# A transformer chain on one core: LayerNorm of the wide attention and of the router, taken as centred weights and a scale

## The chip, the cores and the metric

One core of a Trainium2 chip runs the whole program. The metric is the time on the device in microseconds (us), from one launch; smaller is better. The engines are TensorE (PE; its weight loads are listed as PEld), VectorE (DVE), ScalarE (ACT), GpSimd (POOL) and SyncE (SP, which here issues most DMAs).

## The reference, cut to what matters

32 samples of 128 tokens with 256 features pass through four pairs of cross attention and feed-forward. Each block takes the LayerNorm of the state (no gain, no offset) and is added with a gate:

```python
def _layernorm(x, axis=-1, eps=1e-05):
    m = jnp.mean(x, axis=axis, keepdims=True)
    v = jnp.var(x, axis=axis, keepdims=True)
    return (x - m) / jnp.sqrt(v + eps)

x = x + tanh(g_xattn[1]) * _L1_xattn_ref(_layernorm(x), ctx, w_q, w_k, w_v, w_out, b_out)
x = x + tanh(g_ffn[1])   * _L1_ffn_ref(_layernorm(x), router_w, router_b, expert_w, expert_b)
```

The wide attention (L1) has 16 heads of 64: queries `norm(x) @ w_q`, keys and values from the context, `softmax(q k^T / 8)`, then the output matrix. The mixture behind it picks one of eight experts per token: `logits = norm(x) @ router_w + router_b`, its softmax maximum is the weight, and the chosen expert's matrix is applied to `norm(x)`.

## The kernel before, in words

Four lanes (one sample each) run interleaved. A lane goes through the stages L0 (narrow cross attention), bit (a ternary feed-forward with a convolution), L1 (wide attention) and route (the router) for its 8 passes; then through mix, L2, self and L3 for 8 passes; at the end eight lanes run the last feed-forward. Each stage is written per engine as a generator whose `yield`s cut it into turns, and one string per engine (`ORDER`) says which lane has the next turn. So the order on each engine is fixed, and an engine that waits in one turn holds up every later turn of all lanes. The strings come from a planner outside the kernel.

A LayerNorm (`dve_norm`) is `st` and `ag` on DVE (mean and variance), `var` and `rstd` on POOL (lines 1464 and 1466), then `xn` on DVE (line 785): `(x - mean) * rstd`. PE transposes `xn` (`pe_normed`, the helper's line is 403), ACT copies the result to `xnT`, and the matmuls use that.

In L1 a lane does two halves of eight heads: scores in two PSUM banks, DVE's maximum over 128x1024 (line 839) and `shift` (line 842), eight exponentials on ACT (line 1346, each 128x128 with the row sum as accumulator), a reciprocal per four heads on DVE (`rc`, line 847), the normalisation on POOL (`n`, line 1506), the transposes on PE (line 423), values, output matrix, and an add to the state (`x0`, `x1`, line 854). The exponential and its shift are:

```python
dve.tensor_scalar(top, top, -WIDE ** -0.5, None, ALU.mult)
last = act.activation(t.e[half][:, j, :], t.ab[:, half, j * S:(j + 1) * S], ACT.Exp, scale=WIDE ** -0.5,
                      bias=t.tiny[:, 8 + h:9 + h], accum_out=t.tiny[:, 40 + h:41 + h])
```

In route, `xn` is used twice: by the router's matmul, whose logits get the bias in `lg` (line 950), and by the experts, for which SP sends it to DRAM (`mixture_in`, line 1736). The semaphore `kept` counts the DMAs of the state and of `mixture_in`; the next pass's L0.xn on DVE and L0 `xb` on POOL wait for it, since they overwrite `xn` and `x`. The next pass's keys on PE may start once `lg` has read its bank.

In some passes a lane also computes a tile of the experts (`pe_tile`, `dve_norm`'s `tile.y`) inside these stages. The set-up's constants are turns of a fifth lane; lane 0 starts after them, since its second bank serves as their PSUM bank (`setup_bank`). Up to `bias_L1` they prepare the ternary weights and the output matrices.

## Time and profile before

| | us |
|---|---|
| timed runs, median of 3 | 2629.39 (2628.02 to 2634.43) |
| profiled execution | 2608.25 |
| its span from first to last instruction | 2607.0 |
| PE busy in the span | 2456.1 (94%) |
| DVE busy | 2012.0 (77%) |
| ACT busy | 1666.9 (64%) |
| POOL busy | 1136.2 (44%) |

Busy times are of the profiled execution, whose time is 21 us under the median of the timed runs. Matmuls are pipelined and their ends are modelled, so a busy PE is not a PE at its peak. The first half (L0, bit, L1, route) lies before about 1230 us, the second half behind it, with an overlap of some tens of us.

### The profile page before, as it was taken

To read this page: it belongs to the slowest core of one execution; us is meant where nothing else is said; L and a number is where in the kernel's file an instruction comes from. 1 tells how busy PE (TensorE), PEld (TensorE's weight loads), DVE (VectorE), ACT (ScalarE), POOL (GpSimd) and SP (SyncE) were. 2 spreads that over 40 slices of the span, in tenths; PEclk is the share of its full clock that TensorE was granted. 3 is DMA by queue.
4 is the path that set the end of the run, shared out by engine and by line. 5 is a ranking of instruction groups with operands and counts; after the bars stand their busy time and mean duration, and the time that the engine had idled before them with its cause. 6 is when DMAs were issued, how large, how long until landed. Compare 5 with 4: busy or idle time off the path is not lost.

```text
span 2607.0 us, 66544 instructions
## 1 busy us (share of the span) xinstructions
PE 2456.1 (94%) x26500; PEld 2019.9 (77%) x26500; DVE 2012.0 (77%) x4666; ACT 1666.9 (64%) x4539; POOL 1136.2 (44%) x1989
## 2 busy tenths in 40 slices
PE   6898989898899989999999999999999999999999
PEld 5687867687677777787778878788887878788887
DVE  7778787878688695977586667778777676868998
ACT  4676766777676766676566566666666565656544
POOL 3233423333544544334654554434343433345776
PEclk8898989999999999999999999999999999999999
DMA  6000000000011221000011321100000100000111
GB/s 204 6 24 9 22 10 26 10 20 16 22 48 58 74 60 50 26 24 22 26 55 43 92 76 42 40 20 20 12 27 16 29 16 23 26 6 11 45 32 35
DMA packets 84189, 92.50 MB, mean 35 GB/s; under 512 B 15332, under 2 KB 77288, under 8 KB 83880
## 3 DMA queue, kind: packets, MB, share of 16 engines
q1 hardware_dynamic: 75432, 59.91, 7.4%
q0 software_dynamic: 8448, 28.34, 3.8%
q8 instruction: 210, 3.44, 0.6%
q14 instruction: 99, 0.81, 0.1%
HBM read 65.36 MB, written 22.85 MB: 34 GB/s over the span
## 4 chain that ended last, share of the span: by engine, by line
PE 57%; DVE 23%; ACT 7%; POOL 7%; issue 4%; DMA 2%; SPq 0%; DVEq 0%; POOLq 0%; ACTq 0%
PE psum L375 13%; PE psum L368 10%; PE psum L452 6%; PE psum L403 6%; PE psum L423 5%; DVE tiny L801 3%; PE psum L468 3%; PE psum L596 3%; DVE big L810 3%; PE psum L382 2%; PE psum L396 2%; PE psum L389 2%; PE psum L590 2%; DVE big L891 2%; DVE xn L785 2%
## 5 line engine op out<-in xcount | busy, mean ns | idle before, releaser
L1303 ACT ACTIVATE big<-big 128x512 f32<-128x512 f32 x512 | 313.0, 630 | 155.7 <-DVE big L810 153.3
L801 DVE TENSOR_REDUCE tiny<-psum 128x8 f32<-128x1024 f32 x256 | 311.3, 1219 | 61.0 <-PE psum L452 58.5
L1464 POOL TENSOR_SCALAR tiny<-mv 128x1 f32<-128x1 f32 x224 | 53.4, 238 | 672.2 <-DVE mv L775 670.4
L810 DVE TENSOR_TENSOR big<-psum,tiny 128x512 f32<-128x512 f32 x512 | 335.7, 682 | 4.6
L452 PE MATMUL psum<-head_keys,small 64*128 64x256 f32 x2048 | 286.6, 402 | 17.1 <-ACT big L1265 8.0
L423 PEld LDWEIGHTS psum<-ident,big 64*128 64x128 f32 x5120 | 206.7, 141 | 104.5 <-ACT big L1303 33.1
L423 PE MATMUL psum<-ident,big 64*128 64x64 f32 x5120 | 246.3, 232 | 37.6 <-POOL big L1506 18.6
L1481 POOL TENSOR_TENSOR head_keys<-big,head_rows 128x512 f32<-128x512 f32 x256 | 266.2, 1051 | 0.3
L1265 ACT ACTIVATE big<-psum 128x512 f32<-128x512 f32 x384 | 212.2, 600 | 57.6 <-PE psum L423 54.4
L1506 POOL TENSOR_TENSOR big<-big,tiny 128x512 f32<-128x512 f32 x128 | 134.9, 1058 | 224.5 <-DVE tiny L847 224.2
L452 PEld LDWEIGHTS psum<-head_keys,small 64*128 64x128 f32 x2048 | 182.1, 191 | 63.2 <-ACT big L1265 17.8
L1346 ACT ACTIVATE big<-psum,tiny 128x128 f32<-128x128 f32 x512 | 181.1, 380 | 28.0 <-DVE tiny L842 27.5
L403 PE MATMUL psum<-ident,small 128*128 128x128 f32 x896 | 157.6, 285 | 12.5 <-DVE small L819 4.3
L1265 ACT ACTIVATE head_keys<-psum 128x512 f32<-128x512 f32 x256 | 140.5, 598 | 37.2 <-PE psum L423 36.1
L785 DVE TENSOR_SCALAR xn<-x,mv,tiny 128x256 f32<-128x256 f32 x192 | 103.4, 539 | 74.7 <-POOL tiny L1466 73.8
L403 PEld LDWEIGHTS psum<-ident,small 128*128 128x128 f32 x896 | 100.7, 142 | 51.1 <-DVE small L819 10.9
L1466 POOL TENSOR_TENSOR tiny<-tiny,minus_half 128x1 f32<-128x1 f32 x224 | 129.8, 579 | 18.6
L368 PE MATMUL psum<-xnT,w_L 128*128 128x128 f32 x1024 | 129.7, 277 | 0.8 <-ACT xnT L1333 0.6
L368 PE MATMUL psum<-xnT,w_up 128*128 128x128 f32 x1024 | 130.0, 278 | 0.1
L596 PE MATMUL psum<-w_L,head_keys 128*128 128x256 f32 x512 | 129.0, 390 | 0.7 <-ACT head_keys L1355 0.5
L368 PEld LDWEIGHTS psum<-xnT,w_L 128*128 128x128 f32 x1024 | 123.4, 192 | 5.4 <-ACT xnT L1333 1.9
L368 PEld LDWEIGHTS psum<-xnT,w_up 128*128 128x128 f32 x1024 | 121.3, 192 | 2.8 <-issue 0.9
(339 smaller groups left out, 6473.9 us busy)
## 6 DMA issues: line engine op xcount, KB each, us to landing
ctxT<-in_ctxT SPq DMA_DIRECT2D x64, 128.0 KB, 2.3
after_L_xattn<-x SPq DMA_DIRECT2D x64, 128.0 KB, 1.7
mixture_out<-spare SPq DMA_DIRECT2D x46, 128.0 KB, 2.0
x_in<-in_x SPq DMA_DIRECT2D x32, 128.0 KB, 2.2
mixture_in<-xn SPq DMA_DIRECT2D x32, 128.0 KB, 1.7
x_in<-after_L_xattn SPq DMA_DIRECT2D x32, 128.0 KB, 2.1
w_bits<-after_L_xattn SPq DMA_DIRECT2D x32, 128.0 KB, 2.1
spare<-in_L_w SPq DMA_DIRECT2D x2, 1024.0 KB, 7.2
```

The lines of the kernel that those rows point to most:

```text
L368: last = pe.matmul(bank[:, j * S:(j + 1) * S], wt[:, k, n * P:(n + 1) * P], src[:, k, :], start=k == 0, stop=k == KD - 1)
L375: last = pe.matmul(bank[:, 0:n], srcT[:, k, :], wt[:, k, 0:n], start=k == 0, stop=k == chunks - 1)
L403: last = pe.transpose(bank[:, k * P:(k + 1) * P], src[:, k * P:(k + 1) * P], identity)
L423: last = pe.transpose(t.ab[:, half, at:at + P // 2], t.e[c][rows, j, :], m.ident[rows, rows])
L452: last = pe.matmul(t.ab[:, half, cols], t.qT[rows, r, :], keys[rows, cols], start=l != "self", stop=l != "self" or cols.start > 0)
L596: last = pe.matmul(t.b[:, 0:D], t.kT_wide[:, k, :], m.w["L1o"][:, CH * r + k, :], start=k == 0, stop=k == CH - 1)
L801: dve.tensor_reduce(top, s8, AX.X, ALU.max).then_inc(*t.dve.tell(p, f"{l}.top{r}"))
L810: dve.tensor_tensor(t.e[half], s8[:, mine, :], top[:, mine].rearrange("p (h o) -> p h o", o=1).to_broadcast([P, CH, S]), ALU.subtract).the ...
L1265: return act.activation(dst.rearrange("p h (r s) -> p h r s", r=2), src, ACT.Copy)
L1303: last = act.activation(flat, flat, ACT.Exp, scale=DH ** -0.5)
L1346: last = act.activation(t.e[half][:, j, :], t.ab[:, half, j * S:(j + 1) * S], ACT.Exp, scale=WIDE ** -0.5, bias=t.tiny[:, 8 + h:9 + h], ac ...
L1481: pool.tensor_tensor(t.head_keys[r], t.kT[:, r:r + 1, :].to_broadcast([P, CH, S]), m.head_rows[:].rearrange("p (h o) -> p h o", o=1).to_br ...
```

## The change

The LayerNorm of L1 and of route is no longer applied to the tokens. At set-up PE sums each column of the query matrix and of the router over its 256 rows (a matrix of ones times the weights: `sum_q0`, `sum_q1`, `sum_r`), and DVE subtracts the column's mean from the weights (`mid_q0`, `mid_q1`, `mid_r`), so that the mean of a token drops out of the product. PE then transposes the state `x` itself (`pe_direct`, after `bit.x` or `L1.x1`). The deviation is applied later: in L1 as the exponential's scale, a [128, 1] tensor with rstd / 8 (POOL multiplies the variance by 64 first), and in `shift`; in route as a factor in `lg`. L1's `xn` on DVE is gone; that of route, which the experts need, moves behind `one`, the last step of the router. POOL's `xb` of L1 waits for PE's transposes of `x` instead of `xn`. Where L1 carries a tile, its `tile.y` comes behind `ag` as before, and PE waits for it ahead of the queries. Lane 0 starts after `mid_r` instead of `bias_L1`; the other lanes' first L1 waits for `mid_q1`.

The order strings of all engines are written anew. Counted in turns along them: on PE three more (3627 for 3624), on DVE 29 fewer (3934 for 3963); most turns stand within 10 places of where they stood, once the fewer turns of DVE are counted off. Distance from L1's last output to the router's transposes on PE: median 7 turns before, 4 now; from the router's matmul to the lane's next L0 keys 5 before, 7.5 now; from L1's scores to their transposes 11 before and now; on DVE from route.xn to the lane's next L0.xn 14 to 41 (median 21) before, 4 to 21 (median 7.5) now, in five of 28 places 4 or 5.

```diff
STAGE = {
     "L1": {
         "pe": "kv0 xnT q0 s0 T0 pv0 out0 q1 kv1 s1 T1 pv1 out1",
-        "dve": NORM["dve"] + " top0 shift0 rc0 rc1 x0 top1 shift1 rc2 rc3 x1",
+        "dve": "st ag top0 shift0 rc0 rc1 x0 top1 shift1 rc2 rc3 x1",
         "act": "k0 v0 xnT q0 p0 p1 eT0 eT1 oT0 q1 k1 v1 p2 p3 eT2 eT3 oT1",
         "pool": NORM["pool"] + " xb n0 n1 n2 n3",
     },
...
     },
     "route": {
         "pe": "xnT rt",
-        "dve": NORM["dve"] + " lg mx sub hot hmx one",
+        "dve": "st ag lg mx sub hot hmx one xn",
         "act": "xnT ex",
         "pool": NORM["pool"] + " inv wt",
     },
...
     "pool": "var rstd " + " ".join(f"hb{b} var{b} rstd{b}" for b in range(BLOCKS)),
 }
 SETUP = {
-    "pe": "o_L0 mean o_L1",
-    "dve": "ident fold_L0 bias_L0 abs clip deq r1 r2 r3 w1 s1 s2 w2 fold_L1 bias_L1 plan",
+    "pe": "o_L0 mean o_L1 sum_q0 sum_q1 sum_r",
+    "dve": "ident fold_L0 bias_L0 abs clip deq r1 r2 r3 w1 s1 s2 w2 fold_L1 bias_L1 mid_q0 mid_q1 mid_r plan",
     "act": "tanh",
     "pool": "fill diag band consts first grid",
 }
...
 
 ORDER = {
     "pe": (
...
     ),
     "dve": (
...
     ),
     "act": (
...
     ),
     "pool": (
...
     ),
     "sp": (
...
     ),
 }
 
...
     yield
 
 
+def pe_direct(pe, m, t, p, l, before):
+
+    pe.wait_ge(*t.dve.at(p, before))
+    transposes(pe, t.a, t.x, KD, m.ident[:]).then_inc(*t.pe.tell(p, f"{l}.xnT"))
+    yield
+
+
 def pe_cross(pe, m, t, p, l):
     if l == "L0":
         pe.wait_ge(t.loaded_c, 16 * p + 16)
...
     yield
     pe.wait_ge(*t.act.at(p, f"{l}.v0"))
     yield from pe_tile(pe, m, t, p, l)
-    yield from pe_normed(pe, m, t, p, l)
+    yield from pe_direct(pe, m, t, p, l, "bit.x")
     pe.wait_ge(*t.act.at(p, f"{l}.xnT"))
+    if tile_of(t.n, p, l):
+        pe.wait_ge(*t.dve.at(tile_of(t.n, p, l)[2], "tile.y"))
     for r in range(2):
         chunks = range(CH * r, CH * (r + 1))
         features_T(pe, t.a if r else t.b, m.w["L1q"], t.xnT, chunks[:2])
...
 
 
 def pe_route(pe, m, t, p, l):
-    yield from pe_normed(pe, m, t, p, l)
+    yield from pe_direct(pe, m, t, p, l, "L1.x1")
     if p == 0:
-        pe.wait_ge(m.loads["router"], m.loaded["router"])
+        pe.wait_ge(*m.s.dve.at(0, "setup.mid_r"))
     pe.wait_ge(*t.act.at(p, f"{l}.xnT"))
     tokens(pe, t.b, t.xnT, m.w["router"], E1).then_inc(*t.pe.tell(p, f"{l}.rt"))
     yield
...
 
 def pe_lane(pe, m, t):
     if t.n == 0:
-        pe.wait_ge(*m.s.dve.at(0, "setup.bias_L1"))
+        pe.wait_ge(*m.s.dve.at(0, "setup.mid_r"))
     for p in range(PASSES_A):
         yield from pe_cross(pe, m, t, p, "L0")
         if p == 0:
             pe.wait_ge(*m.s.dve.at(0, "setup.w2"))
         yield from pe_bitlinear(pe, m, t, p, "bit")
         if p == 0:
-            pe.wait_ge(*m.s.dve.at(0, "setup.bias_L1"))
+            pe.wait_ge(*m.s.dve.at(0, "setup.mid_q1"))
         yield from pe_wide(pe, m, t, p, "L1")
         yield from pe_route(pe, m, t, p, "route")
     for p in range(PASSES_A):
...
     pe.wait_ge(*m.s.dve.at(0, "setup.fold_L1"))
     pe_fold(pe, m, "L1", m.setup_bank).then_inc(*m.s.pe.tell(0, "setup.o_L1"))
     yield
+    for n, before in enumerate(("bias_L1", "mid_q0")):
+        pe.wait_ge(*m.s.dve.at(0, f"setup.{before}"))
+        for k in range(KD):
+            last = pe.matmul(m.setup_bank, m.ones[:], m.w["L1q"][:, k, n * BANK:(n + 1) * BANK],
+                             start=k == 0, stop=k == KD - 1)
+        last.then_inc(*m.s.pe.tell(0, f"setup.sum_q{n}"))
+        yield
+    pe.wait_ge(m.loads["router"], m.loaded["router"])
+    pe.wait_ge(*m.s.dve.at(0, "setup.mid_q1"))
+    for k in range(KD):
+        last = pe.matmul(m.setup_bank[:, 0:E1], m.ones[:], m.w["router"][:, k, :], start=k == 0, stop=k == KD - 1)
+    last.then_inc(*m.s.pe.tell(0, "setup.sum_r"))
+    yield
 
 
 def pe_lora(pe, m, t, p, l):
...
     yield
 
 
+def dve_moments(dve, t, p, l):
+
+    dve.bn_stats(t.stats[:], t.x[:]).then_inc(*t.dve.tell(p, f"{l}.st"))
+    yield
+    dve.wait_ge(*t.dve.at(p, f"{l}.st"))
+    dve.bn_aggr(t.mv[:], t.stats[:]).then_inc(*t.dve.tell(p, f"{l}.ag"))
+    yield
+
+
 def dve_wide(dve, m, t, p, l):
-    yield from dve_norm(dve, m, t, p, l, t.x[:], t.xn[:])
+    yield from dve_moments(dve, t, p, l)
+    if tile_of(t.n, p, l):
+        k = tile_of(t.n, p, l)[2]
+        dve.wait_ge(*t.pe.at(k, "tile.y"))
+        dve.tensor_tensor(t.xg, t.b[:, 0:D], t.bg, ALU.add).then_inc(*t.dve.tell(k, "tile.y"))
+        yield
     s8 = t.ab.rearrange("p r (h s) -> p (r h) s", s=S)
     top = t.tiny[:, 8:16]
     for r in range(2):
...
         dve.tensor_reduce(top, s8, AX.X, ALU.max).then_inc(*t.dve.tell(p, f"{l}.top{r}"))
         yield
         dve.wait_ge(*t.dve.at(p, f"{l}.top{r}"))
-        dve.tensor_scalar(top, top, -WIDE ** -0.5, None, ALU.mult).then_inc(*t.dve.tell(p, f"{l}.shift{r}"))
+        dve.wait_ge(*t.pool.at(p, f"{l}.rstd"))
+        dve.tensor_scalar(top, top, t.tiny[:, 1:2], -1.0, ALU.mult, ALU.mult).then_inc(*t.dve.tell(p, f"{l}.shift{r}"))
         yield
         for half in range(2):
             mine = t.tiny[:, 40 + CH * half:40 + CH * (half + 1)]
...
         dve.wait_ge(*t.dve.at(p, f"{l}.{name}"))
 
     dve.wait_ge(*t.dve.at(p, "L1.x1"))
-    yield from dve_norm(dve, m, t, p, l, t.x[:], t.xn[:])
+    yield from dve_moments(dve, t, p, l)
     if p == 0:
         dve.wait_ge(m.loads["router"], m.loaded["router"])
         dve.wait_ge(*m.s.dve.at(0, "setup.plan"))
     dve.wait_ge(*t.pe.at(p, f"{l}.rt"))
-    yield from then(dve.tensor_tensor(lg, t.b[:, 0:E1], m.w["rb"][:], ALU.add), "lg")
+    dve.wait_ge(*t.pool.at(p, f"{l}.rstd"))
+    yield from then(dve.scalar_tensor_tensor(lg, t.b[:, 0:E1], t.tiny[:, 1:2], m.w["rb"][:], ALU.mult, ALU.add), "lg")
     yield from then(dve.tensor_reduce(mx, lg, AX.X, ALU.max), "mx")
     yield from then(dve.tensor_scalar(lg, lg, mx, None, ALU.subtract), "sub")
     yield from then(dve.scalar_tensor_tensor(wt, lg, 0.0, m.first_of[:], ALU.is_equal, ALU.mult), "hot")
     yield from then(dve.tensor_reduce(mx, wt, AX.X, ALU.max), "hmx")
     dve.tensor_scalar(m.hots[sample // MIX][:, sample % MIX, :], wt, mx, None, ALU.is_equal
                       ).then_inc(*t.dve.tell(p, f"{l}.one"))
+    yield
+    dve.tensor_scalar(t.xn[:], t.x[:], t.mv[:, 0:1], t.tiny[:, 1:2], ALU.subtract, ALU.mult
+                      ).then_inc(*t.dve.tell(p, f"{l}.xn"))
     yield
 
 
...
     dve_fold(dve, m, "L1").then_inc(*m.s.dve.tell(0, "setup.fold_L1"))
     yield
     dve_bias(dve, m, "L1")
+    yield
+    for n in range(2):
+        dve.wait_ge(*m.s.pe.at(0, f"setup.sum_q{n}"))
+        for k in range(KD):
+            mine = w["L1q"][:, k, n * BANK:(n + 1) * BANK]
+            last = dve.scalar_tensor_tensor(mine, m.setup_bank, -1.0 / D, mine, ALU.mult, ALU.add)
+        last.then_inc(*m.s.dve.tell(0, f"setup.mid_q{n}"))
+        yield
+    dve.wait_ge(*m.s.pe.at(0, "setup.sum_r"))
+    for k in range(KD):
+        last = dve.scalar_tensor_tensor(w["router"][:, k, :], m.setup_bank[:, 0:E1], -1.0 / D, w["router"][:, k, :],
+                                        ALU.mult, ALU.add)
+    last.then_inc(*m.s.dve.tell(0, "setup.mid_r"))
     yield
     dve.wait_ge(*m.s.pool.at(0, "setup.grid"))
     dve.tensor_scalar(m.before[:], m.causal[:], 0.0, None, ALU.is_le)
...
             act.wait_ge(*t.dve.at(p, f"{l}.shift{r}"))
             for j in range(CH):
                 h = CH * half + j
-                last = act.activation(t.e[half][:, j, :], t.ab[:, half, j * S:(j + 1) * S], ACT.Exp, scale=WIDE ** -0.5,
+                last = act.activation(t.e[half][:, j, :], t.ab[:, half, j * S:(j + 1) * S], ACT.Exp, scale=t.tiny[:, 1:2],
                                       bias=t.tiny[:, 8 + h:9 + h], accum_out=t.tiny[:, 40 + h:41 + h])
             last.then_inc(*t.act.tell(p, f"{l}.p{2 * r + half}"))
             yield
...
 
 def pool_rstd(pool, m, t, p, l, sub=""):
     pool.wait_ge(*t.dve.at(p, f"{l}.ag{sub}"))
-    pool.tensor_scalar(t.tiny[:, 0:1], t.mv[:, 1:2], LN_EPS, None, ALU.add).then_inc(*t.pool.tell(p, f"{l}.var{sub}"))
+    of = WIDE if l == "L1" else 1
+    pool.tensor_scalar(t.tiny[:, 0:1], t.mv[:, 1:2], LN_EPS, of, ALU.add, ALU.mult
+                       ).then_inc(*t.pool.tell(p, f"{l}.var{sub}"))
     pool.wait_ge(*t.pool.at(p, f"{l}.var{sub}"))
     pool.tensor_tensor(t.tiny[:, 1:2], t.tiny[:, 0:1], m.minus_half[:], ALU.pow
                        ).then_inc(*t.pool.tell(p, f"{l}.rstd{sub}"))
...
 def pool_wide(pool, m, t, p, l):
 
     yield from pool_rstd(pool, m, t, p, l)
-    pool.wait_ge(*t.dve.at(p, f"{l}.xn"))
+    pool.wait_ge(*t.pe.at(p, f"{l}.xnT"))
     pool.tensor_tensor(t.x[:], t.x[:], m.out_bias[l][:], ALU.add).then_inc(*t.pool.tell(p, f"{l}.xb"))
     yield
     for c in range(4):
```

## Rows read from the trace of the kernel before

**Rows 1.** The page's first part: busy us (share of the span) and instructions.

```profile
PE 2456.1 (94%) x26500; PEld 2019.9 (77%) x26500; DVE 2012.0 (77%) x4666; ACT 1666.9 (64%) x4539; POOL 1136.2 (44%) x1989
```

**Rows 2.** Length, busy us of PE, PEld, DVE, ACT, POOL; clock, DMA, GB/s.

```profile
100.00:1230.00 1130.00, 1049.98 (x12221) 854.77 (x12220) 893.36 (x2318) 781.94 (x2416) 449.27 (x679) 0.98 0.10 30
1230.00:2607.00 1377.00, 1336.99 (x13661) 1113.70 (x13658) 1042.62 (x2169) 836.08 (x2003) 661.44 (x1234) 1.00 0.11 33
```

**Rows 3.** The same, by slices of the first half.

```profile
326.00:391.00 65.00, 57.93 (x643) 45.53 (x640) 57.13 (x141) 41.76 (x114) 16.17 (x26) 0.89 0.03 10
...
456.00:522.00 66.00, 57.72 (x674) 46.18 (x673) 58.89 (x158) 47.52 (x140) 20.70 (x32) 0.97 0.03 10
522.00:587.00 65.00, 63.81 (x802) 52.60 (x801) 49.93 (x123) 47.20 (x154) 23.67 (x36) 1.00 0.07 20
```

**Rows 4.** Waits, 100 to 1230 us: waiting line <- releaser, total, times, longest.

```profile
DVE xn L785 <- POOL tiny L1466: 46.4, 41, 4.5
...
DVE tiny L847 <- ACT big L1346: 31.1, 39, 2.5
...
PE psum L423 <- POOL big L1506: 18.6, 19, 6.3
```

**Rows 5.** Groups by form, to 1230 us: count, busy, mean ns, idle before.

```profile
L785 DVE TENSOR_SCALAR xn<-x,mv,tiny 128x256 f32<-128x256 f32 x102 | 53.5, 526 | 42.8 <-POOL tiny L1466 42.1
...
L403 PE MATMUL psum<-ident,xn 128*128 128x128 f32 x200 | 41.9, 293 | 18.6 <-DVE xn L785 13.1 <-ACT small L1259 4.1 <-ACT small L1325 0.5
```

**Rows 6.** In time, one router of lane 1: start, us, what, idle.

```profile
138.32 0.41 DVE L854 TENSOR_TENSOR x<-psum,x 128x256 f32<-128x256 f32 x1
...
139.88 0.57 POOL L1466 TENSOR_TENSOR tiny<-tiny,minus_half 128x1 f32<-128x1 f32 x1
...
140.48 0.41 DVE L785 TENSOR_SCALAR xn<-x,mv,tiny 128x256 f32<-128x256 f32 x1 [0.43 <-POOL tiny L1466]
...
140.92 0.33 SPq L1736 DMA_DIRECT2D mixture_in<-xn  x1
...
141.57 0.38 PE L403 MATMUL psum<-ident,xn 128*128 128x128 f32 x2
...
143.65 0.16 DVE L950 TENSOR_TENSOR tiny<-psum,w_rb 128x8 f32<-128x8 f32 x1
```

**Rows 7.** DMA issues: count, KB each, us to landing.

```profile
mixture_in<-xn SPq DMA_DIRECT2D x32, 128.0 KB, 1.7
```

**Rows 8.** ACT by form, in time, in the chain: one and two tensor operands.

```profile
L1346 ACT ACTIVATE big<-psum,tiny 128x128 f32<-128x128 f32 x512 | 181.1, 380 | 28.0 <-DVE tiny L842 27.5
...
L1446 ACT ACTIVATE big<-psum,beta,gamma 128x128 f32<-128x128 f32 x96 | 38.2, 456 | 24.4 <-PE psum L403 24.2
...
363.03 0.62 ACT L1252 ACTIVATE small<-psum,w_L0bq 128x128 f32<-128x128 f32 x2
...
363.69 2.91 ACT big L1346 x16
...
2451.14 1.50 ACT L1446 ACTIVATE small<-psum,beta,gamma 128x128 f32<-128x128 f32 x4
```

**Rows 9.** ACT busy in line 1346 alone, in slices of rows 3.

```profile
326.00:391.00 65.00, 5.99 (x33) 0.89 0.03 10
...
456.00:522.00 66.00, 7.70 (x43) 0.97 0.03 10
...
sum 261.00, ACT 44.68; mean ACT 11.17
```

**Rows 10.** Set-up: by 10 us, lane 0's start, a DVE operation.

```profile
50.00:60.00 10.00, 9.46 (x115) 7.48 (x106) 9.42 (x32) 4.60 (x13) 3.48 (x8) 1.00 0.01 3
60.00:70.00 10.00, 3.09 (x30) 2.22 (x30) 10.00 (x34) 5.95 (x14) 1.24 (x3) 0.72 0.00 0
...
53.63 0.61 PE L382 MATMUL psum<-ctxT,w_L0k 128*128 128x128 f32 x4
...
L1062 DVE SCALAR_TENSOR_TENSOR big<-big,psum 128x512 f32<-128x512 f32 x64 | 43.1, 678 | 20.6 <-ACT big L1410 20.5
```

More of the change, by code:

```diff
@@ new lines @@
+        "0301200103312202321003110310301101201203313321112100120120322032031131313133122300120022222123312312"
+        "1313333033121023102001133221310232131030220232332113131023020200000003320213212033013032030320101221"
+        "2211001333003110121112110021012210203203202030331103223321300110012122212233213233131033032213203112"
+        "2001303200211031233120310212302000110122100023303232320203232101301013312023221030311310002011333310"
+        "0211021112110021032022302030113223123211212213322322113300002312331212332303310123120203132103123321"
@@ new lines @@
+        "0321300101221332113031022312020202003302320103123220312311300310311002302101020133020320123120021012"
+        "1211200111303201203030311032100300312123323121222101230131303131010330300311223100201221321221201021"
+        "2133021023211331122300032000330223323020312012002123011332201221310110331303033120312301203322003301"
+        "1121211001201302302020303311202300302132222112212301203113012101230312310332323112033213022311200212"
+        "0121332313322300211301100000003302232302132012033001322110220331010313013030001123333100211102112100"
@@ L243 @@
[L243 to L245 removed]
+        "2331203012141311324322141441343232214144442124113031412112112414242121323212131030303131313010113111"
+        "0231323313130303231313231331000322222010230203202202332232301100122132200000013120301001113101101310"
@@ new lines @@
+        "2120100230333213101202011320321113302232310231211200100332320231030332101311201200302210232331331032"
+        "1202200131301022132022313301300210311212210030220123132131323001230203013123120231230313300120011112"
+        "2223200630073763763389969767880779868967ab09679a7bab80800066a779bba89786976ab8a979b6876a799ab8a4565b"
+        "b9574a4968a8695b4b7548aa455b48b8a5945a9b5ab44b865865b94a747a9b564584869545ba75b64489a79576b454868abb"
+        "5454a9a978567a6545b4a8947967b6a55a4848bb5544"
@@ L300 @@
+        "230330310300221313102120213232300102010112230323301001202160323171328233005011122a011342b322143c3030"
+        "2090031012212230311033024001421432304034211122303204011034321233041041221230443001289387ab87a7ca70bc"
+        "9896ba58cc6b5c6a56599879b67a58a7cb965bc65"
     ),
```

230 lines of the change are left out of this document (105 added, 125 removed).

## The prediction

> **What bounds the kernel now.** First the page's busy shares: TensorE (PE) 94%, VectorE (DVE) 77%, ScalarE (ACT) 64% of the span [rows 1]. These average over stages with different limits, so next the table by stretch [rows 2]. The change touches only the set-up and the stages L1 and route, which lie before about 1230 us. From 100 to 1230 us PE stands idle 1130 - 1050 = 80 us, DVE is busy 893 us (79%) and ACT 782 us (69%). From 1230 us on PE idles only 40 us of 1377; there I expect nothing but small shifts from the new order. Then the slices of about 65 us [rows 3]. Two kinds alternate: in one, DVE is busy 57 to 59 us and PE idles 7 to 8 us; in the other DVE is busy about 50 us and PE idles about 1 us. So in one half of the slices DVE is the co-bound and a microsecond taken off it can count; in the other half PE hides it.
>
> The waits say which DVE time is idle [rows 4]. In this stretch DVE waits 46.4 us in 41 places for POOL's rstd before an `xn`, 31.1 us in 39 places for ACT's exponentials before a reciprocal. PE waits 18.6 us in 19 places for POOL's normalisation, which stands behind those exponentials, and 13.1 us for an `xn` [rows 5]. All this is in-order: an engine that waits in one lane's turn holds up the other three lanes' turns behind it.
>
> **Removed: the `xn` of L1.** By form, the 102 `xn<-x` of the window cost 53.5 us busy (526 ns each) and 42.1 us of idle time for rstd [rows 5]. They are 32 each of bit, L1 and route and 6 of the second half. Pro rata, the 32 of L1 take 32 x 0.526 = 16.8 us of work, and L1 and route together 64/102 x 42.1 = 26.4 us of waiting. The new L1 needs rstd only at `shift0`, after keys, queries, scores and the maximum; the new route needs it at `lg`. In the example of the router [rows 6], x1 starts at 138.32 us, `xn` at 140.48, the transposes at 141.57 and `lg` at 143.65; rstd was issued at 139.88 and lasts 0.57, and is there at 140.45. The transposes would start right after x1 (138.73) and `lg` 2.1 us later, near 140.8: rstd comes in time, but not by much. Waits and L1 work: 16.8 + 26.4 = 43 us of DVE time over the stretch.
>
> **Moved: the `xn` of route.** It stays (0.53 us each, so no work saved) and goes behind `one`. Its work there lies outside the lane's chain. What hangs on it is the DMA of `mixture_in` on SP's queue and then `kept`, for which DVE's next L0.xn and POOL's next L0 `xb` wait. In the new strings 4 to 21 DVE turns (median 7.5) lie between route.xn and the next L0.xn; before it was 14 to 41. One DVE instruction comes every 1130/2318 = 0.49 us, so the median distance is 3.7 us and the shortest 2.0 us, against issue 0.33 + landing 1.7 = 2.0 us [rows 6, 7]. Only five of 28 places have 4 or 5 turns. I take +1 us; bounds 0 and 28 us, 1 us (half of that way) in each place, if SP stands at another lane's wait when a route.xn ends.
>
> **Added: the scale as a tensor operand in 512 exponentials.** The trace before has no such Exp. Nearest rows [rows 8]: an ACT instruction from PSUM with 128 columns and one such operand (today's Exp, with its bias) lasts 380 ns, with two (scale and bias, the Gelu) 456 ns. In distance, two with one operand take 0.62 us, so about 0.25 apart; four with two operands take 1.50 us, so (1.50 - 0.456)/3 = 0.35 apart. Eight exponentials with their accumulator reads take 2.91 us today. So +0.08 to +0.10 us each; I take 0.10, the distance: 512 x 0.10 = 51 us more on ACT, which goes from 69 to 74% and does not become the bound. What matters is latency: the transposes of a half-bank wait for all eight exponentials, so +0.8 us per group, 16 groups per lane. The Trainium skill (ScalarE: Activation LUTs, section "What ACT_TABLE_LOAD costs") gives about 93 ns for each pointer operand; by it ACT would get 512 x 0.093 = 48 us, an estimate beside the 51 us; no run here shows Exp with both yet.
>
> Where does this count? PE already stalls in 19 places behind this chain; if each grows by 0.8 us: +15 us. At the other end 0, where the order has other lanes' work. By slice, 31% of the exponentials' time ((5.99 + 7.70)/44.68) lies in the slices with DVE at its limit [rows 9]; elsewhere PE has work. I take a third, +5 us. The DVE reciprocals wait for four exponentials, 0.4 us more in 39 places: 16 us of DVE idle, 31% of it, 5 us, in the slices where DVE counts.
>
> **Added: set-up.** Two bank sums of two matmuls with 512 columns each. In the row of lane 0's start, two matmuls of 128 columns (four entries, two for each fp32 matmul) take 0.61 us [rows 10]; by columns that makes 4 x 0.61 = 2.4 us for a bank. Each is followed by two DVE operations of 0.68; then come the router's small ones, about 1 us. On DVE that is 4 x 0.68 + 2 x 0.16 = 3.0 us, at a time when DVE is busy 9 to 10 us of every 10 [rows 6, 10]. In a chain: 2 x (2.4 + 1.36) + 1.0 = 8.5 us, for which lane 0 waits after `bias_L1`; it began at 53.63 us. But PE is nearly idle from 60 to 70 us (3.09 busy), so a later lane 0 fills part of a hole. I take DVE's 3 us; bounds 0 and 8.5.
>
> Edits at nothing: `shift` and `lg` with a tensor scalar (a 0.2 us instruction stays one), POOL's factor in the same instruction, PE's transposes (same count, other source). L1's `xb` on POOL now waits for PE's transposes instead of `xn`; POOL is idle 60% of the stretch and hides it; with that cover gone rstd of other lanes would come late and the waits of [rows 4] would come back.
>
> **The sum.** DVE: half of 43 us falls in slices where it counts, 21.5, less 5 for the reciprocals: -16.5. Exponentials +5, set-up +3, L0.xn +1: -7.5 us. Against the profiled execution's 2608.25 us: 2600.8. The median of the timed runs is 2629.4, 21 us above that execution; the difference carried over gives 2622.
>
> A second way, by one lane's chain: each pass saves the way from the end of x1 (138.73) to the end of `xn` (140.89), 2.2 us, and pays 2 x 0.8 = 1.6 us in L1's exponentials [rows 6, 8]: 0.6 us per pass, over 8 passes 5 us less. Same sign and size.
>
> **Rivals.** (1) The DVE gain is eaten: PE's turns keep almost the same sequence (L1's scores to its transposes 11 turns before and after, next L0 keys 5 turns behind the router before, 7.5 after), so the planner found nothing for an earlier router to feed. Then the 43 us become other waits. What is left: 5 + 3 + 1 = 9 us of costs against PE's own stalls on `xn`, 13.1 us for 100 transposed tiles, 64 of them in L1 and route: 8 us [rows 5]. That gives +1: 2630. For it: PE 93% busy; against: the DVE-heavy slices.
>
> (2) The whole 43 us counts. 43 - 9 of costs = -34: 2595. For it speaks that in the stretch PE's weight loads are busy only 855 of 1130 us, 76%. [...] Against it: slices with PE at 63.8 of 65.
>
> (3) Slower: the exponentials decide. If PE stalls 0.8 us in half of the 64 groups (it stalls in 19 places today) that is +26 us, with the other terms -16.5 + 26 + 4 = +14: 2643. From 16 full stalls on the sum is a loss. For it: L1's half-bank chain is the largest cause of PE waits; against: 69% of it lies where PE is full of other lanes.
>
> (4) Slower: L0.xn waits for `kept` about 0.6 us in each of 28 passes, +17 instead of +1: 2638.
>
> **Numbers.** A difference under 0.3% (8 us) can't be told from none. Forecast, a small gain around 2622 (2612 to 2629): 0.46, of which 0.27 is beyond 0.3%. Rival 1: 0.18 (0.04 of it slower). Rival 2: 0.15. Rival 3: 0.15. Rival 4: 0.06. Faster 0.27 + 0.15 = 0.42; same 0.19 + 0.14 = 0.33; slower 0.04 + 0.15 + 0.06 = 0.25. The range reaches into rivals 2 and 3: 2597 to 2645.
>
> **What would show it.** In the profile after: the 32 `xn` of L1 gone, and DVE's wait for rstd down from 46 to about 20 us; the exponential at about 460 ns, 0.45 apart; DVE's wait for exponentials up from 31 to 40 to 50 us; lane 0 beginning near 62 us; PE idle in 100 to 1230 us down from 80 to about 70. I am wrong if PE's stalls behind the normalised exponentials grow beyond 35 us, if DVE waits for a landing before L0.xn, or if the exponential does not get longer.

## The result: slower by 2.1%, and the profile after

The changed kernel takes 2686.98 us (2686.41 to 2692.09 over three runs) against 2629.39: ratio 1.021, interval 1.0188 to 1.0232. That is 55 us more where 7.5 us less were forecast, and it lies outside the range.

The first profiled execution of before (span 2607.0 us) was a short one. A second trace of the same kernel, taken with the experiments, spans 2627.8 us, close to its timed median of 2629.37; where times are compared by stage, this second trace stands for before. The first part of its page, and of the page of after (span 2685.1 us):

```profile
PE 2466.0 (94%) x26500; PEld 2024.9 (77%) x26500; DVE 2012.9 (77%) x4666; ACT 1669.0 (64%) x4539; POOL 1138.8 (43%) x1989
```

```profile
PE 2482.0 (92%) x26512; PEld 2035.4 (76%) x26512; DVE 2002.6 (75%) x4640; ACT 1710.6 (64%) x4539; POOL 1118.3 (42%) x1989
```

DVE has 10 us less to do, ACT 42 us more. PE is busy 16 us longer and idles 203 us of its span instead of 162. The windows of after that answer to [rows 2, 3] (columns as there):

```profile
100.00:1230.00 1130.00, 1011.24 (x11553) 819.32 (x11555) 836.64 (x2214) 788.66 (x2315) 415.14 (x630) 0.97 0.10 29
...
326.00:391.00 65.00, 55.27 (x644) 44.45 (x647) 55.32 (x139) 47.35 (x136) 23.65 (x41) 0.94 0.06 20
456.00:522.00 66.00, 58.51 (x712) 48.34 (x704) 47.58 (x137) 46.04 (x133) 23.93 (x43) 0.97 0.07 23
522.00:587.00 65.00, 59.24 (x685) 48.27 (x683) 53.84 (x141) 49.22 (x146) 20.25 (x30) 0.97 0.05 15
```

PE idles 1130 - 1011 = 119 us, not 80 (86 in the second trace of before). In the slice from 522 to 587 us, where before had PE full (63.81 of 65), it idles 5.8 us, and 9.7 and 7.5 in the other two, where it was 7.1 and 8.3 (the work in them is some 20 us behind that of before): in that slice the cover on which the prediction counted is gone. DVE's and PE's waits from 100 to 1230 us, which answer to [rows 4]:

```profile
DVE tiny L884 <- ACT big L1400: 78.0, 76, 4.8
DVE tiny L875 <- PE psum L583: 33.5, 20, 10.4
...
DVE xn L807 <- POOL tiny L1522: 7.1, 11, 1.0
```

```profile
PE psum L423 <- ACT big L1400: 15.5, 16, 3.4
PE psum L583 <- ACT head_keys L1392: 8.5, 7, 5.6
PE psum L368 <- ACT xnT L1331: 8.0, 7, 1.7
PE psum L403 <- DVE xn L807: 7.2, 7, 2.9
PE psum L423 <- POOL big L1562: 5.9, 11, 1.4
```

DVE's wait for rstd before an `xn` is nearly gone (46.4 to 7.1 us; 3.6 us of it came back at the logits, in 5 places), as forecast. In its place DVE stands 78 us, in 76 places, behind the exponentials (31.1 in 39 before). PE's own stalls at the transposes of the exponentials (its line 423, released by ACT or by POOL) are as small as they were, 15.5 + 5.9 = 21.4 us (21.8 and 15.6 in the two traces of before); its idle time is now spread over many short waits for ACT. The exponentials, by form, and one half-bank's run in time:

```profile
L1400 ACT ACTIVATE big<-psum,tiny 128x128 f32<-128x128 f32 x512 | 227.9, 470 | 29.6 <-DVE tiny L879 29.1
...
L1400 ACT ACTIVATION_READ_ACCUMULATOR big<-psum,tiny 128x1 f32 x512 | 111.4, 218 | 0.0
```

```profile
167.56 0.46 ACT L1400 ACTIVATE big<-psum,tiny 128x128 f32<-128x128 f32 x1
...
167.99 0.46 ACT L1400 ACTIVATE big<-psum,tiny 128x128 f32<-128x128 f32 x1
...
168.43 0.47 ACT L1400 ACTIVATE big<-psum,tiny 128x128 f32<-128x128 f32 x1
```

They last 470 ns (380 before) and start 0.43 apart: 46.8 us more on ACT (227.9 - 181.1). In the set-up (PE, in time) the three sums and then lane 0's start:

```profile
57.25 1.98 PE L733 MATMUL psum<-w_L,ones 128*128 128x512 f32 x4
...
60.62 1.98 PE L733 MATMUL psum<-w_L,ones 128*128 128x512 f32 x4 [0.52 <-DVE w_L L1208]
...
64.08 0.58 PE L740 MATMUL psum<-w_router,ones 128*128 128x8 f32 x4
...
64.99 0.71 PE L382 MATMUL psum<-ctxT,w_L0k 128*128 128x128 f32 x4
```

Lane 0 begins at 64.99 us instead of 53.63 [rows 10]. A router of after, in time, answers to [rows 6]:

```profile
152.85 0.38 PE L403 MATMUL psum<-ident,x 128*128 128x128 f32 x2
...
154.07 0.51 PE L375 MATMUL psum<-w_router,xnT 128*128 128x8 f32 x4
...
154.31 0.55 POOL L1522 TENSOR_TENSOR tiny<-tiny,minus_half 128x1 f32<-128x1 f32 x1
...
155.00 0.23 DVE L988 SCALAR_TENSOR_TENSOR tiny<-psum,tiny,w_rb 128x8 f32<-128x8 f32 x1 [0.70 <-POOL tiny L1522]
```

The transposes no longer wait for rstd, but here the logits do, 0.70 us.

By stage (from the starts of the routers' matmuls in the traces): the fourth router of pass 1, that of pass 8, and the end.

| | pass 1 | passes 2 to 8 | behind | end |
|---|---|---|---|---|
| before, first trace | 215 | 996 | 1396 | 2607 |
| before, second trace | 214 | 1012 | 1402 | 2628 |
| after | 230 | 1041 | 1414 | 2685 |
| after, constant scale (below) | 223 | 1007 | 1413 | 2644 |

So of 57 us, 16 lie before the fourth router of pass 1, 29 in the seven passes, 12 behind. Two traces of the same kernel differ by 16 us in the seven passes, so a split of single traces is no finer than that.

### The profile page after: what moved, and what is told of

Read it like the earlier page. It is cut to its first block, busy times and chain, and to the rows that moved or that the text cites. A ratio compares the mean times of both kernels' runs of the same rounds, so it can differ in the third digit from the quotient of the medians.

```text
span 2685.1 us, 66646 instructions
## 1 busy us (share of the span) xinstructions
PE 2482.0 (92%) x26512; PEld 2035.4 (76%) x26512; DVE 2002.6 (75%) x4640; ACT 1710.6 (64%) x4539; POOL 1118.3 (42%) x1989
## 4 chain that ended last, share of the span: by engine, by line
PE 52%; DVE 21%; ACT 14%; POOL 5%; issue 4%; DMA 2%; another core or an unknown queue 1%; SPq 0%; DVEq 0%; POOLq 0%; ACTq 0%
PE psum L375 12%; PE psum L368 9%; ACT big L1400 6%; PE psum L452 6%; PE psum L403 6%; PE psum L423 5%; DVE tiny L823 3%; PE psum L468 3%; DVE big L832 3%; PE psum L605 2%; PE psum L396 2%; PE psum L382 2%; PE psum L389 2%; PE psum L599 2%; DVE big L928 1%
## 5 line engine op out<-in xcount | busy, mean ns | idle before, releaser
L1519 POOL TENSOR_SCALAR tiny<-mv 128x1 f32<-128x1 f32 x224 | 46.5, 208 | 673.7 <-DVE mv L797 473.7
L423 PE MATMUL psum<-ident,big 64*128 64x64 f32 x5120 | 249.4, 234 | 38.9 <-ACT big L1400 15.5
L1400 ACT ACTIVATE big<-psum,tiny 128x128 f32<-128x128 f32 x512 | 227.9, 470 | 29.6 <-DVE tiny L879 29.1
L375 PE MATMUL psum<-w_down,big 128*128 128x256 f32 x512 | 121.3, 383 | 0.4 <-DVE big L1103 0.2
```

The source lines that it names most:

```text
L375: last = pe.matmul(bank[:, 0:n], srcT[:, k, :], wt[:, k, 0:n], start=k == 0, stop=k == chunks - 1)
L423: last = pe.transpose(t.ab[:, half, at:at + P // 2], t.e[c][rows, j, :], m.ident[rows, rows])
```

## Experiments

Differences are taken by ratio (1% is 26 us) against the runs of before made beside each kernel.

**The second operand, taken out and put in alone.** In the changed kernel a constant scale; in the kernel before a tensor scale that holds the same 1/8.

```
-  ACT.Exp, scale=t.tiny[:, 1:2], ...          # changed kernel
+  ACT.Exp, scale=WIDE ** -0.5, ...
-  dve.tensor_scalar(top, top, t.tiny[:, 1:2], -1.0, ALU.mult, ALU.mult)
+  dve.tensor_scalar(top, top, -WIDE ** -0.5, None, ALU.mult)

-  ACT.Exp, scale=WIDE ** -0.5, ...            # kernel before
+  ACT.Exp, scale=m.wide_scale[:], ...
```

> The changed kernel, but the exponentials of L1 take the constant 1/8 as their scale, and shift multiplies by the constant too (the row's deviation is left out of L1's softmax). Order, set-up, transposes and waits stay. Theory: the second tensor operand is what costs; the exponential goes back from 470 to about 380 ns, DVE's wait for exponentials from 81 to about 35 us, and the time falls from 2687 to 2635-2645 us (the set-up's share stays). Rival 'order': the route's later xn and the new order cost the time; then it stays within 10 us of 2687 although the exponential is short again.

> The kernel before with one edit: the exponentials' scale is read from a 128x1 tensor that holds 1/8, so nothing changes in the result. Theory: exponential 380 to 470 ns and the time goes up by 35 to 50 us, to 2665-2680 us, because nothing is gained on DVE in exchange. My prediction's sizing (a third of the stalls, +5 to +10 us with the reciprocals) would give 2635-2640; rival 'order': under 2640 as well.

Measured: the first 2644.11 us, ratio 1.0037 (1.0021 to 1.0052); the second 2661.15, ratio 1.01 (1.0078 to 1.0123). By form, the exponential of the changed kernel with the constant, then that of the kernel before with the tensor:

```profile
L1400 ACT ACTIVATE big<-psum,tiny 128x128 f32<-128x128 f32 x512 | 181.6, 383 | 28.1 <-DVE tiny L879 27.7
```

```profile
L1346 ACT ACTIVATE big<-psum,tiny,wide_scale 128x128 f32<-128x128 f32 x512 | 228.2, 470 | 26.6 <-DVE tiny L842 26.2
```

DVE's waits for them, 100 to 1230 us, in the same two kernels:

```profile
DVE tiny L884 <- ACT big L1400: 42.9, 53, 4.5
```

```profile
DVE tiny L847 <- ACT big L1346: 60.6, 68, 2.9
```

The operand costs (1.021 - 1.0037) x 2630 = 45 us in the new order, about ACT's 46.8, and 26 us in the old one, under the 35 to 50 expected there. The rival 'order' falls as the main cause. But without the operand the change still loses 10 us, although DVE is freed of all that it was to be freed of; its seven passes (1007 us) lie between the two traces of before.

How these microseconds reach PE can be summed from the traces of the two kernels and of these two runs, from 100 us to the last router's matmul (the waits over all rows of PE):

| | length | PE busy | PE waits for ACT | for DVE | for POOL |
|---|---|---|---|---|---|
| before, second trace | 1126 | 1040 | 31 | 35 | 13 |
| before, tensor scale | 1152 | 1052 | 50 | 31 | 10 |
| after, constant scale | 1131 | 1039 | 55 | 22 | 9 |
| after | 1172 | 1050 | 81 | 25 | 6 |

With the operand PE waits 18 and 26 us more for ACT (for the exponentials, and for copies that ACT makes for other turns), and it is busy 11 us longer with the same matmuls. The mean granted clock of TensorE in these four executions is 0.980, 0.978, 0.980 and 0.976, so part of the price may be the clock; no run holds it fixed. PE's waits for DVE hardly changed (5 us less, 3 more). Whether ACT's copies are late because the exponentials before them last longer, or because the lanes behind a DVE that stands are late, these sums do not tell.

**The set-up's work left out, and both edits together.** The sums and subtractions are cut to 8 columns.

```
-  for k in range(KD): last = pe.matmul(m.setup_bank, m.ones[:], m.w["L1q"][:, k, ...BANK], ...)
+  last = pe.matmul(m.setup_bank[:, 0:E1], m.ones[:], m.w["L1q"][:, 0, ...E1], start=True, stop=True)
-  last = dve.scalar_tensor_tensor(mine, m.setup_bank, -1.0 / D, mine, ALU.mult, ALU.add)
+  last = dve.scalar_tensor_tensor(mine, m.setup_bank[:, 0:E1], 0.0, mine, ALU.mult, ALU.add)
```

> The changed kernel with the set-up's bank sums and subtractions cut to one matmul of 8 columns and one subtraction of 8 columns times zero each (the weights stay uncentred, so L1's and the router's inputs keep their mean); all waits and signals stay. Theory: lane 0 begins about 8 us earlier and the time falls by 5 to 10 us, to about 2679. If PE's empty stretch in the set-up hides it: under 3 us.

> The changed kernel with both edits, constant scale and no centring (leaves out the row's deviation in L1's softmax and the centring). If the two costs are separate, the gain is the sum of the two single ones, and what is left against 2629 is the worth of the order and the moved xn. Theory: 2625-2635 us. Rival 'order': it stays above 2670.

Measured: 2693.63, ratio 1.0219 (1.0198 to 1.0239), and 2646.98, 1.005 (1.0033 to 1.0067). Nothing is gained by smaller set-up work, so 'under 3 us' holds, and both edits together give what the constant scale gives alone, not the 2625 to 2635 expected. In the trace of the first of the two runs lane 0 still begins at 62.33 us. The size of the work is not the cost. Whether its turns are is the next run's question.

**The set-up alone, in the kernel before** (the changed kernel's turns with the factor 0, lane 0 waiting for them).

```
-  if t.n == 0: pe.wait_ge(*m.s.dve.at(0, "setup.bias_L1"))
+  if t.n == 0: pe.wait_ge(*m.s.dve.at(0, "setup.mid_r"))
+  last = dve.scalar_tensor_tensor(mine, m.setup_bank, 0.0, mine, ALU.mult, ALU.add)
```

> The kernel before with the change's set-up alone: the three bank sums on PE and the six subtractions on DVE, all for which lane 0 now waits, at the places nearest to those of the new strings that have no deadlock, with the factor 0 in place of -1/256, so that the weights stay as they are. Nothing is left out. My prediction's sizing: lane 0 begins 5 to 8 us later and the time grows by 3 us (0 to 8.5). From the trace after (the first routers 9 us later even with a constant scale): 5 to 10 us. None left at the end: within 3 us of 2630.

Measured: 2641.3, ratio 1.0038 (1.0024 to 1.0053): 10 us, with lane 0 at 61.61 us, 8 later than in [rows 10]. Most of the delay of the first lane is carried on: against the second trace of before the fourth router and the last are each 6 us later, the end 12. PE's hole takes up 2 us of it at most.

**L1's part alone and the route's alone, in the order of before.** In L1 the `xn` turn becomes empty and the transposes read x; in route the router is centred, the transposes read x, `xn` follows `one`. Then the route part once more with `xn` right behind `lg`.

```
-  yield from pe_normed(pe, m, t, p, l)                       # L1
+  yield from pe_direct(pe, m, t, p, l, "bit.x")
-  "dve": NORM["dve"] + " lg mx sub hot hmx one"              # route
+  "dve": "st ag lg mx sub hot hmx one xn"
-  "dve": "st ag lg mx sub hot hmx one xn"                    # route, third run
+  "dve": "st ag lg xn mx sub hot hmx one"
```

> The kernel before, unchanged, for a second trace of it: its first profiled execution was 21 us under the median of its timed runs. Expected: about 2630 us as in the timed runs; the trace then shows in which stretch the first one was shorter.

> Of the change L1's part alone, in the order strings of before and without its two costs: L1's tokens are transposed straight from x, its xn is gone (its turn is empty), the exponentials keep the constant scale; the centring and the row's deviation are left out of L1. It shows what the removed xn and its wait are worth. Prediction's sizing (half of 17 us of work and 13 us of waiting): about 2615 us. Theory 'eaten': 2625-2634, with DVE's other waits up by as much as the removed work and wait.

> Of the change the route part alone, in the order strings of before: the router's weights centred in the set-up, its tokens transposed straight from x, rstd taken in at the logits, xn behind the one-hot turn; L1 keeps its xn and its constant scale. Prediction's sizing (half of 13 us of waiting counts): about 2624 us. Theory 'eaten' (lanes wait for PE's results anyway): 2627-2634. Rival 'late xn' (the next L0.xn waits for the copy of this xn): 2640 or more, with DVE or POOL waiting for mixture_in's landing.

> The route part alone, as in the earlier run (2639.8 us, DVE waiting 7.5 us in 8 places for the copy of xn before the next L0.xn), with xn right behind the logits instead of behind the one-hot turn, five turns earlier. Nothing is left out. If the late xn is what the route part costs: DVE's waits for that copy go from 7.5 us to under 2 and the time to 2630-2633. Rival (the cost is the longer way from the router's matmul to the logits and the set-up's extra turns): 2636-2642 although those waits go.

Measured: before again 2629.37 (1.0004, 0.9991 to 1.0018); L1's part 2635.57, ratio 1.0024 (1.0014 to 1.0034); the route part 2639.82, 1.004 (1.0025 to 1.0056); with the earlier `xn` 2641.08, 1.004 (1.0026 to 1.0054). Each half of the gain, alone and free of the operand, makes the kernel slower, by 6 and 10 us; the first is less than the 0.3% from which the prediction would tell a difference, but neither is a gain. In the route run DVE's waits for rstd fall from 42.2 us (second trace of before) to 22.1, and this appears:

```profile
DVE xn L798 <- DMA mixture_in<-xn: 7.5, 8, 2.1
```

The `xn` that comes late is waited for in 8 places; with the earlier `xn` that row is gone, and the time is the same. So 'late xn' falls as the cause of the 10 us; the rival's 2636 to 2642 came, but its two reasons were not tested apart.

Where the freed DVE time goes shows in DVE's waits for PE. First L1's part, then the route's, each with the same line in the second trace of before above it:

```profile
DVE x L854 <- PE psum L596: 22.1, 20, 5.0
DVE x L878 <- PE psum L605: 29.1, 21, 5.4
```

```profile
DVE tiny L950 <- PE psum L375: 8.9, 10, 3.1
DVE tiny L973 <- PE psum L375: 14.1, 15, 3.8
```

Over all rows, from 100 us to the last router, DVE waits for PE 121.8 us in the second trace of before, 139.8 with L1's part and 139.0 with the route's: 17 to 18 us more, while its waits for POOL fall from 44.5 to 38.4 and 23.6. A single place shows the same, DVE's order around the first plan (690 to 703 us). First the second trace of before, then the route run:

```profile
687.65 0.41 DVE L785 TENSOR_SCALAR xn<-x,mv,tiny 128x256 f32<-128x256 f32 x1 [4.54 <-POOL tiny L1466]
700.91 1.23 DVE L839 TENSOR_REDUCE tiny<-psum 128x8 f32<-128x1024 f32 x1 [12.84 <-remote]
```

```profile
703.11 1.23 DVE L861 TENSOR_REDUCE tiny<-psum 128x8 f32<-128x1024 f32 x1 [17.85 <-remote]
```

The wait of 4.54 us for rstd is taken away, and the next instruction's wait grows from 12.84 to 17.85 (what releases that instruction the profile does not name). What else makes the route part slower than no change is not settled.

**The reciprocals of L1 moved in DVE's string**, in the changed kernel, nothing else; back by up to two turns, then ahead by up to two (a turn is some 0.5 us).

```
-  "dve": ... shift0 rc0 <turn of another lane> <turn of another lane> ...
+  "dve": ... shift0 <turn of another lane> <turn of another lane> rc0 ...     # and the mirror
```

> The changed kernel with one edit of DVE's order string: each of L1's 128 reciprocals is moved back behind up to two turns of other lanes (118 by two, 5 by one, 5 not at all). Nothing is left out. Theory 'misplaced' (the order puts the reciprocals where the shorter exponentials would have ended, so all lanes stand behind them): DVE's wait for exponentials falls from 78 to under 50 us and the time by 10 to 25 us, to 2662-2677. Rival 'latency' (the longer exponentials hold up their own lane's transposes whatever DVE does): within 5 us of 2687, or slower.

> The mirror of the run with the later reciprocals: in the changed kernel's DVE string each reciprocal of L1 is moved ahead of up to two turns of other lanes (107 by two, 17 by one, 4 not at all). Theory 'chain': DVE stands longer behind exponentials (over 100 us) and the time still falls or stays, 2665-2690. Theory 'DVE's stalls are the cost': over 2700.

Measured: later 2758.76, ratio 1.0491 (1.0463 to 1.0519), 74 us over the changed kernel; earlier 2790.84, 1.0593 (1.0569 to 1.0617), 101 us over it. With later reciprocals PE waits (first row below, that run), with earlier ones DVE (second, the mirror):

```profile
PE psum L423 <- POOL big L1562: 61.5, 51, 3.9
```

```profile
DVE tiny L884 <- ACT big L1400: 145.9, 92, 4.8
```

The theories 'misplaced' and 'chain' fall. With later reciprocals DVE's wait for exponentials is down to 8.8 us, and the time grows all the same, as 'latency' allowed; with earlier ones it comes out over 2700, as 'DVE's stalls are the cost' had it. So the turns stand neither too early nor too late, and neither wait is the cost by itself: later, each half-bank's transposes are late and with them PE, which serves all lanes in a fixed order; earlier, DVE stands and with it all lanes.

Part of the price is TensorE's clock. The windows from 100 to 1230 us of the later and of the earlier reciprocals, to be compared with that of after (clock 0.97):

```profile
100.00:1230.00 1130.00, 982.28 (x10868) 793.23 (x10870) 806.37 (x2107) 742.19 (x2171) 390.11 (x596) 0.93 0.09 28
```

```profile
100.00:1230.00 1130.00, 962.70 (x10656) 778.64 (x10657) 791.36 (x2051) 731.39 (x2128) 390.19 (x591) 0.93 0.09 28
```

A matmul is busy 90 ns on average there, 87.5 in after; over the whole span PE idles 241 and 268 us instead of 203, and the same 26512 matmuls take 2520 and 2524 us instead of 2482. About 40 us of each of the two losses are PE's own work at a lower granted clock.

**Reciprocals made by POOL**, in both kernels: the DVE turns go, POOL raises the sums to -1 itself.

```
-  pool.wait_ge(*t.dve.at(p, f"{l}.rc{c}"))
+  pool.wait_ge(*t.act.at(p, f"{l}.p{c}"))
+  pool.tensor_tensor(mine, mine, m.minus_one[:].to_broadcast([P, CH]), ALU.pow)
```

> The kernel before with L1's 128 reciprocals taken off DVE: POOL raises the row sums to the power -1 itself (0.57 to 0.60 us) in the turn in which it normalises; nothing is left out. Theory 'chain' (what counts is the way from the scores through exponentials, reciprocal and normalisation to the transposes, in all lanes): DVE's wait for exponentials (31 us) is gone, the chain of a half-bank is about as long as before or a little shorter, and the time falls by 5 to 20 us, to 2610-2625. Rival 'DVE's freed time is eaten': 2627-2635. Slower (over 2640) if POOL's 73 us of extra work delays other lanes' rstd.

> The changed kernel with the same edit, reciprocals by POOL. DVE stands 78 us behind exponentials there, so if those stalls cost the time, this gives back 20 to 35 us: 2652-2667. If it is the length of the chain and not DVE's stalls, it gives about what it gives in the kernel before, 5 to 20 us.

Measured: 2712.03, ratio 1.0306 (1.0289 to 1.0322), and 2747.97, 1.0452 (1.0434 to 1.0469): 80 and 64 us more, though DVE's waits for exponentials are gone altogether. In the kernel before so edited:

```profile
PE psum L422 <- POOL big L1504: 64.8, 64, 2.5
```

```profile
L1501 POOL TENSOR_TENSOR tiny<-tiny,minus_one 128x4 f32<-128x4 f32 x128 | 132.8, 1037 | 176.1 <-ACT big L1340 175.9
```

PE waits in 64 places, 18.6 us in 19 before [rows 4]. POOL's reciprocal of 128x4 lasts 1037 ns, not the 0.57 to 0.60 us that I had read from its instructions of 128x1, so the way from the scores to the transposes is longer by some 0.87 us in 128 places (DVE's reciprocal lasts 0.17): 111 us, of which 80 and 64 show in the time. So taking DVE's stalls away gains nothing where that way gets longer. DVE's waits for rstd grew too, from 42.2 to 53.7 us in the kernel before; the run does not part the two.

**The old strings behind the last router**, then SP's old string as well.

```
   ORDER["pe"], ["dve"], ["act"], ["pool"]: new up to lane 0's first turn behind its last router, then as before
+  ORDER["sp"]: as before
```

> The changed kernel, whose order strings of PE, DVE, ACT and POOL from lane 0's first turn behind its last router on are those of before (SP's string stays new). Nothing is left out. The trace after takes 1414 us from the last router to the end, the second one of before 1402. Theory: the new strings cost that, and the time falls by 6 to 12 us, to 2675-2681. Rival: the second half is longer for another reason (the granted clock, where the lanes stand when it begins): under 3 us.

> The changed kernel with all of before's order behind the last router, as in the run before, and the order string of SP (the queue of loads and stores) of before as a whole. Nothing is left out. The way from the last router to the end was 1414 us with either string on the other engines, 1402 in the kernel before. If SP's new order costs it: 1402-1405 us there, and about 2668-2673 in all. Otherwise: no difference to 2680.

Measured: 2680.31, ratio 1.0181 (1.0156 to 1.0207), and 2679.77, 1.0192 (1.0169 to 1.0214). Both intervals overlap the changed kernel's. The stage behind the last router stays at 1414 us with the first edit and is 1405 with the second, but the last router is later by as much (1272 us against 1263). So the 12 us there stay unexplained.

**A shorter chain: no maximum in L1's softmax**, in both kernels; then in the kernel before with a tensor scale.

```
-  dve.tensor_reduce(top, s8, AX.X, ALU.max) ; dve.tensor_scalar(top, ...)      # 2 turns a half-bank
-  act.activation(..., ACT.Exp, scale=..., bias=t.tiny[:, 8 + h:9 + h], accum_out=...)
+  act.activation(..., ACT.Exp, scale=..., accum_out=...)
```

> The kernel before with L1's maximum and its shift left out of DVE (128 turns): the exponentials take no bias, which leaves the softmax's result as it is as long as nothing overflows. The way from the scores to the exponentials gets shorter by the maximum and the shift, 1.22 + 0.15 us in 64 half-banks (88 us), and DVE has 88 us less work. Theory 'chain, both ways': a shorter chain counts like a longer one, about one to one with what was seen for longer ones (60 to 90%): 50 to 80 us less, 2550-2580. Theory 'the order has fixed it' (turns stand where they were planned; a shorter step turns into waiting, only a longer one is felt): 2610-2632.

> The changed kernel with the same edit; the exponentials keep the deviation as their scale, but lose the bias, so they have one tensor operand again. If the change's loss is the second operand in that chain, it has to vanish here: the difference to the run before it (the kernel before without the maximum) should shrink from 57 us to 10-15 us, about 14 to 16 of set-up and second half less what the first half gains. If it stays above 40 us, the second operand is not the cause.

> The kernel before without L1's maximum (as two runs ago), and with the exponentials' scale read from a 128x1 tensor that holds 1/8; the result stays. It has the one operand in the exponentials that the changed kernel without the maximum has too, in the order of before. Theory: this operand is the whole difference between the two (2607.8 and 2629.2): 2625-2632. Rival: with a shorter chain there is slack for it, under 2615, and the rest of the difference is the order and the set-up.

Measured: 2607.82, ratio 0.9912 (0.99 to 0.9925); 2629.23, 0.9987 (0.9975 to 0.9999); 2620.65, 0.9952 (0.9938 to 0.9966). The exponentials by form, of the first and of the last:

```profile
L1337 ACT ACTIVATE big<-psum 128x128 f32<-128x128 f32 x512 | 134.6, 299 | 3.5 <-remote 3.2 <-PE psum L573 0.3
```

```profile
L1337 ACT ACTIVATE big<-psum,wide_scale 128x128 f32<-128x128 f32 x512 | 181.5, 388 | 0.0
```

DVE waits for them 22.4 us in 24 places in the first and 39.8 in 43 in the last.

88 us off the chain (and off DVE) give 23 us, far from one to one and just beyond what 'the order has fixed it' allows: most of what is taken away turns into waiting. With the chain short, the operand costs (0.9952 - 0.9912) x 2630 = 11 us, not 26; of the 20 us between the two kernels (0.9987 - 0.9912), which is more than the 10 to 15 expected, the operand is half, and the set-up's 10 us, measured alone, is as much as the rest. Neither of the two expectations for the last run holds, it lies between them. The kernel before without the maximum beats both kernels; it keeps the softmax as long as no exponential overflows.

## Why the prediction was wrong, by its steps

**Removed xn and waits: the rows right, their worth wrong.** The 32 `xn` and the waits for rstd went (46.4 to 7.1 us, forecast 20). 'Half of 43 us counts' is the first step that failed: alone, in the old order, L1's part gives +6 us and the route's +10 instead of -21.5 together. That a slice shows DVE busy 57 of 65 us does not make DVE's microseconds count: with four lanes in a fixed order, the freed time became waits for PE (17 to 18 us more with either part). Rival 1 had this right, as far as the gain goes. The Trainium skill (Perfetto Trace Analysis, section "Identifying the Most-Contended Engine") would have one optimise the engine with the highest occupancy first, TensorE being judged by its MFU (its share of the peak arithmetic) or its weight loads, which at 76% made DVE the candidate. The runs don't agree here: 88 us less DVE work, together with a shorter chain, gave 23, and L1's and the route's parts, which take the LayerNorm's work and waits off DVE, gave nothing.

**Exponentials: the price right, the share wrong.** 470 ns and 0.43 apart against 460 and 0.45. The step that cost most is 'I take a third': 5 + 5 us were booked, and 45 us (new order) or 26 (old) are what the operand measures. I looked for the cost at PE's transposes, and those stalls did stay small (21.4 us against my alarm at 35), so the test that I had set would have missed it. The waits stood elsewhere: on DVE, whose reciprocals wait for four exponentials each (78 us), and on PE, which waits 81 us for all that ACT makes, 31 before. The prediction weighted DVE's wait by the DVE-heavy slices and gave PE no wait for ACT's copies; the runs with moved reciprocals show that a shift at this step costs whichever engine waits. Which of the two waits carries the price is not shown. Rival 3 named the right cause, the longer exponentials, at too small a price (+26, 2643 in all) and at the wrong place, the transposes. The second way, by one lane's chain, paid 1.6 us a pass for the exponentials and left out that all four lanes' chains stand in one order, at most 4 x 1.6 = 6.4 us: with and without the operand the seven passes take 1041 and 1007 us, 4.9 us a pass apart, and in the old order 1035 and 1012, 3.2 a pass.

In the new strings the same operand costs more. Counted in them, the first reciprocal (`rc0`) stands 4.2 turns behind the first shift (`shift0`) on average, 4.7 before, although the exponentials last longer. That this is why 26 us became 45 was not shown; moving the reciprocals back alone made it worse.

**Set-up: undersized.** +3 with bounds to 8.5; lane 0 forecast near 62 us, seen at 64.99, and 10 us measured alone. The failing step is the hole in PE that was to be filled; it took up 2 us at most, and 8 us of delay became 10 in the time. Smaller matmuls don't help; that the three turns and their hand-overs between PE and DVE remain is the likely reason, which no run shows.

**Late xn of route: right in size.** +1 us forecast, 2.4 us of such waits in 2 places in DVE after: a sign of being wrong that I had named, but too small to matter; rival 4 did not happen.

By ratio, the parts measured alone in the old order (operand, set-up, L1, route) sum to 26 + 10 + 6 + 10 = 52 us, near the 55 of the whole; in the new order without the operand the rest costs 10, not 26. The split is thus good to some 15 us, and that the sum comes so near is in part luck.

| step | forecast, us | measured, us |
|---|---|---|
| DVE freed, L1 and route | -21.5 | +6, +10 |
| longer exponentials, with the reciprocals' waits | +10 | +45 (new order), +26 (old) |
| set-up | +3 | +10 |
| L0.xn behind the copy | +1 | not to be told from 0 |

## What to carry to other kernels

Where several lanes share in-order engines by a written order, look for the chain that all of them pass through and price a longer step in it by its full length times all lanes, a ceiling that these runs stayed under, and not by a third of one engine's stalls: the same 47 us of ACT's time cost 45 us in one order, 26 in another and 11 where the chain had become shorter. Freed time on an engine was worth nothing here where the turns of all lanes kept their order. Before trading a DVE instruction for an operand on ACT, ask which of the two is in that chain: here 17 us of DVE work were bought with 47 us of ACT time in that chain. And set the alarm of a forecast on every engine that waits in the chain, and on all that it waits for, not on the last step alone.

## What the runs showed of the hardware that I had not expected

One tensor operand costs ScalarE about the same whichever it is: the same 128x128 exponential from PSUM took 299 ns with none, 380 to 391 with one (bias or scale) and 470 with both. The Trainium skill (ScalarE: Activation LUTs, section "What ACT_TABLE_LOAD costs") gives 186 ns + 0.833 ns a column and 93 for each such operand, an estimate of 293, 386 and 479; the traces agree within 9 ns.

POOL's power of -1 took 1037 and 1052 ns for 128x4 (in the two kernels) and 571 to 597 ns for 128x1, so its time could not be carried over from one width to the other.

Where PE idled more, its granted clock was lower and the same matmuls (but for 4.5 us of sums in the set-up) lasted longer: 162, 203, 241 and 268 us of idle PE (before, after, later and earlier reciprocals) go with a mean granted clock of 0.980, 0.976, 0.960 and 0.957 and with 2466, 2482, 2520 and 2524 us of busy PE. So in these runs a stall cost more than its own length.

At the first plan, while POOL issues sixteen scatters, DVE and PE stand in the second trace of before: PE 9.78 us and DVE 12.84, although the last scores before it had ended on PE at 692.0; POOL's last issue ended at 699.1. In the first trace, which is 21 us shorter in all, DVE waits 3.39 us at this place and goes on at 693.3 while POOL still issues until 701.0, so the issuing alone does not hold it. What does, the profile names only "remote", and no run here settles it.
